# Cross-attention and quantised feed-forward, float32 on one core: the projection in two blocks side by side with 512-column matmuls, bias terms off TensorE, and another order on VectorE

## What is computed

```python
# x, ctx: (8, 256, 1024) float32
Q = layernorm(x) @ Wq.T + bq              # 1024 -> 1024
K = ctx @ Wk.T + bk
attn = softmax(Q @ K.T / sqrt(1024))      # within each of the 8 batches
x = x + attn @ ctx
w = scales[g_idx] * (where(nibble > 0, 1, -1) - zeros[g_idx])   # 1024 x 1024, from 4-bit codes
x = x + layernorm(x) @ w + bias
```

## Time and profile before

| | before |
|---|---|
| median of 3 runs | 609.89 us (607.79 to 610.23) |
| the profiled execution, its own time | 609.59 us |
| its span, first to last instruction | 607.8 us |
| TensorE busy | 584.0 us, 96% |
| VectorE busy | 380.8 us, 63% |
| ScalarE, GpSimd busy | 189.5 and 190.5 us, 31% each |
| HBM traffic, mean | 133 GB/s |

### The profile page before, as it was taken

The page is one execution under the profiler, slowest core; times in us unless marked ns, Lnnn a source line. Parts: engine busy times, 40 slices in busy tenths (PEclk is TensorE's granted clock), DMA queues, the critical chain, the costliest instruction groups (busy, mean ns, idle before and its releaser), DMA issues.

```text
span 607.8 us, 8093 instructions
## 1 busy us (share of the span) xinstructions
PE 584.0 (96%) x3098; PEld 501.0 (82%) x3098; DVE 380.8 (63%) x640; ACT 189.5 (31%) x346; POOL 190.5 (31%) x136
## 2 busy tenths in 40 slices
PE   7899999899999999989999999988899999999997
PEld 6799999687877877767889899977688888888886
DVE  4794885279678758845102555566787686777442
ACT  5312112210432332222326766654221222132120
POOL 3460000000000000000024877663856426624630
PEclk9999999899999999989999999999899999999999
DMA  8921200040180441405506599896203203310111
GB/s 272 294 71 35 71 1 2 0 139 1 70 310 36 174 173 69 157 19 189 189 3 243 209 324 354 316 420 271 116 2 139 111 39 128 139 70 0 70 69 70
DMA packets 30853, 81.47 MB, mean 134 GB/s; under 512 B 2600, under 2 KB 10800, under 8 KB 28640
## 3 DMA queue, kind: packets, MB, share of 16 engines
q1 hardware_dynamic: 30816, 80.96, 36.6%
HBM read 53.69 MB, written 27.26 MB: 133 GB/s over the span
## 4 chain that ended last, share of the span: by engine, by line
PE 82%; DVE 8%; DMA 3%; ACT 2%; POOL 2%; issue 1%; SPq 1%; DVEq 0%; ACTq 0%
PE bank L1029 25%; PE bank L1031 25%; PE bank L1030 25%; PE bank L1191 2%; PE bank L1040 2%; PE bank L1119 2%; DVE stats L734 1%; DMA wq_stage<-in_L_xattn_Wq 1%; DMA wk_stage<-in_L_xattn_Wk 1%; DVE xT_lo L685 1%; POOL cn_lo L444 1%; DVE wrow L713 1%; DMA xin<-in_x 1%; POOL tT_lo L451 1%; DVE yin L940 1%
## 5 line engine op out<-in xcount | busy, mean ns | idle before, releaser
L1029 PE MATMUL bank<-xT_hi,m_hi 128*128 128x512 f32 x256 | 106.3, 415 | 1.6 <-DVEq L787 1.6
L1030 PE MATMUL bank<-xT_lo,m_hi 128*128 128x512 f32 x256 | 102.1, 399 | 0.0
L1031 PE MATMUL bank<-xT_hi,m_lo 128*128 128x512 f32 x256 | 101.9, 398 | 0.0
L434 POOL TENSOR_TENSOR pairs<-mv,pairs 128x2 f32<-128x2 f32 x16 | 11.1, 695 | 208.2 <-DVE mv L739 207.5
L993 DVE TENSOR_TENSOR xres<-xres,bank 128x512 f32<-128x512 f32 x56 | 38.3, 686 | 48.3 <-PE bank L1031 48.2
L1029 PE MATMUL bank<-wk_hi,wq_hi 128*128 128x342 f32 x192 | 62.7, 327 | 4.9 <-DVE wk_lo L694 2.5
L466 POOL TENSOR_TENSOR l_lo_s<-l_sum_s,l_hi_s 128x512 fp32r<-128x512 f32 x32 | 40.4, 1296 | 73.3 <-DVE l_sum_s L922 71.8
L1030 PE MATMUL bank<-wk_lo,wq_hi 128*128 128x342 f32 x192 | 61.4, 320 | 0.0
L1031 PE MATMUL bank<-wk_hi,wq_lo 128*128 128x342 f32 x192 | 61.2, 319 | 0.0
L451 POOL TENSOR_TENSOR tT_lo<-t_pair,tT_hi 128x1024 fp32r<-128x1024 f32 x16 | 38.2, 2403 | 72.8 <-ACT tT_hi L490 72.8
L1029 PEld LDWEIGHTS bank<-xT_hi,m_hi 128*128 128x128 f32 x256 | 48.8, 190 | 14.0 <-DVEq L787 1.8
(11 more groups left out here) (138 smaller groups left out, 1299.7 us busy)
## 6 DMA issues: line engine op xcount, KB each, us to landing
xin<-in_x SPq DMA_DIRECT2D x8, 1024.0 KB, 6.3
cin<-in_ctx SPq DMA_DIRECT2D x8, 1024.0 KB, 6.8
xres<-in_x SPq DMA_DIRECT2D x8, 1024.0 KB, 11.6
out<-xres SPq DMA_DIRECT2D x15, 512.0 KB, 2.7
right_scratch<-part_hi SPq DMA_DIRECT2D x28, 256.0 KB, 2.2
r_tile<-right_scratch SPq DMA_DIRECT2D x6, 1024.0 KB, 11.4
r_tile<-right_scratch SPq DMA_DIRECT2D x3, 1536.0 KB, 10.1
right_scratch<-part_lo_t SPq DMA_DIRECT2D x16, 256.0 KB, 2.1
```

What stands on the lines that cost most here:

```text
L1029: pe.matmul(out_, a_hi, b_hi, start=start, stop=False, skip_group_check=True)
L1030: pe.matmul(out_, a_hi, b_lo, start=False, stop=False, skip_group_check=True)
L1031: return pe.matmul(out_, a_lo, b_hi, start=False, stop=stop, skip_group_check=True)
```

## The change

Blocks 0 and 1 of the projection run side by side: slice c of block 0, then slice c of block 1, so Wq's block 1 is loaded early and has buffers of its own; later blocks run one by one. M's rows are two segments of 512 columns; the banks go round by three pairs. Wk no longer has the bk columns. The bias terms: ScalarE multiplies each slice of Wk by bq (`times_bq`) into `wk_bq` and each block of Wq by bk (`times_bk`) into `wq_bk`; VectorE adds the eight slices (three wide additions) for u, and reduces each block (`sum_bk`) into `wacc` for w; `w_row` is two matmuls of 512 columns of float32. A slice of Wk from c = 4 on also waits for `times_bq` of slice c - 4. The second x load waits for blocks 0 and 1. In block 7 the x_tr are spread behind slices 3 to 7, and t's first group doesn't wait for `s_cons`; `w_row` does. In the t stage VectorE does `weights` before the six `x_lo`. On ScalarE `t_hi(2, 0)` moves behind two `c_hi`. At the turn `y_apply(0, 1)` moves up between the `c_lo(7, ...)`, `y_stats(1)` behind the loop, `left_sum` s3 and s4 and both `y_apply(1, ...)` between the residuals of batch 7, and `rsqrt(9)` on GpSimd behind the low parts of s2 and s1.

```diff
 SP:
-            first_wq(0, s_wq0)
+            first_wq(0, 0, s_wq0[0])
             for h, done in enumerate((s_wk0, s_wkl[0])):
...
+            first_wq(1, 0, s_wq0[1])
             for c in range(1, NB):
-                if c == 1:
+                if c == 2:
                     for r, row in enumerate((bq, bk)):
...
-                if c == 2:
-                    first_wq(1, s_wql[0])
+                if c == 3:
+                    for b in range(2):
+                        first_wq(b, 1, s_wql[b])
                 if c >= 4:
                     sp.wait_ge(s_wklo, c - 3)
+                    sp.wait_ge(s_wkbq, c - 3)
                 sp.dma_start(wk_stage[c % 4], wk_rows[:, c, :]).then_inc(s_wkl[c % 4], 16)
-            load_wq(1)
+            load_wq(2)
...
+            for b in range(3, NB):
+                sp.wait_ge(s_wqlo, wq_split_count(b - 3, 1))
+                sp.wait_ge(s_wqbk, b - 2)
                 load_wq(b)
+                if b == 3:
+                    sp.wait_ge(s_m, 4)
+                    sp.dma_start(xin[:, 1, :, :], x_rows[1]).then_inc(s_xl[1], 16)
 ScalarE:
+            def times_bq(c):
...
+                act.activation(wk_bq[:, c, :], wk_stage[c % 4], ACT.Copy, scale=bcols[:, 0, c:c + 1]).then_inc(s_wkbq, 1)
+            def times_bk(b):
+                wait(act, s_wacc, b)
+                for c in range(NB):
+                    ins = act.activation(wq_bk[:, c, :], wq_stage[b % 3][:, c, :], ACT.Copy, scale=bcols[:, 1, c:c + 1])
+                ins.then_inc(s_wqbk, 1)
...
             for c in range(1, NB):
                 if c == 3:
                     wq_split(0, 1)
+                    wq_split(1, 1)
                 act.wait_ge(s_wkl[c % 4], 16 * (c // 4 + 1))
+                copy(wk_hi[:, c, :], wk_stage[c % 4]).then_inc(s_wkhi, 1)
+                if c > 1:
+                    times_bq(c - 2)
+            times_bq(NB - 2)
+            times_bq(NB - 1)
+            times_bk(0)
...
-                if b + 1 < NB:
+                if b != 1 and b + 1 < NB:
                     for h in range(2):
-                        wq_split(b + 1, h)
+                        wq_split(max(b + 1, 2), h)
+                if b > 1:
+                    times_bk(b)
...
+                if b == 1:
+                    times_bk(b)
 VectorE:
+            dve.wait_ge(s_wkbq, NB)
+            order.link(dve.tensor_tensor(wk_bq[:, 0:4, :], wk_bq[:, 0:4, :], wk_bq[:, 4:8, :], ALU.add))
+            order.link(dve.tensor_tensor(wk_bq[:, 0:2, :], wk_bq[:, 0:2, :], wk_bq[:, 2:4, :], ALU.add))
+            dve.tensor_tensor(uacc, wk_bq[:, 0, :], wk_bq[:, 1, :], ALU.add).then_inc(s_uacc, 1)
             order.link(dve.tensor_tensor(jcol, bcols[:, 0, :], bcols[:, 1, :], ALU.mult))
             dve.tensor_reduce(bsum[:, 0:1], jcol, AX_X, ALU.add).then_inc(s_cons, 1)
-            def add_u(c):
...
+            def sum_bk(b):
+                dve.wait_ge(s_wqbk, b + 1)
+                dve.tensor_reduce(wacc[:, b * P:(b + 1) * P], wq_bk.rearrange("p c i -> p i c"), AX_X, ALU.add
+                                  ).then_inc(s_wacc, 1)
...
             for b in range(NB):
+                if b != 1 and b + 1 < NB:
+                    wq_split(max(b + 1, 2), 0)
...
+                if b != 1 and b + 1 < NB:
+                    wq_split(max(b + 1, 2), 1)
+                if b != 1:
+                    sum_bk(b)
                 if b == NB - 1:
-                    for u in range(4):
+                    for u in range(6):
                         x_lo(0, u)
+                for n in range(2):
+                    dve.wait_ge(s_mhi, 2 * b + n + 1)
+                    cols = slice(n * HALF, (n + 1) * HALF)
+                    low(m_lo[:, b, cols], m_bank(b, n)[:, :], m_hi[:, b, cols], s_mlo)
+                if b == 1:
+                    sum_bk(b)
...
                     n = NB * p + j
+                    for h in range(2):
+                        if n - 1 - h in GATHER:
+                            weights(GATHER[n - 1 - h], h)
                     if j == NB - 1 and p + 1 < PAIRS:
                         for u in range(NB - 2):
                             x_lo(p + 1, u)
...
                     if b == 1:
                         p_lo(0)
                         invert_sum(0)
+                    if b == B - 2:
+                        y_apply(0, 1)
                     c_lo(b + 1, 2)
                     c_lo(b + 1, 3)
...
                 row_max(b)
-                if b == B - 2:
-                    y_apply(0, 1)
-                if b == B - 1:
-                    y_stats(1)
...
-                if b == B - 1:
-                    y_apply(1, 1)
-                    y_apply(1, 0)
             p_lo(B - 1)
             invert_sum(B - 1)
-            dve.wait_ge(s_cnlo, 4 * B)
-            left_sum(0, "s3")
-            left_sum(0, "s4")
+            y_stats(1)
...
                 if f == 0:
                     added(f, 0)
                     added(f, 1)
-                    for g in range(4):
-                        residual(B - 1, g)
+                    dve.wait_ge(s_cnlo, 4 * B)
+                    left_sum(f, "s3")
+                    residual(B - 1, 0)
+                    left_sum(f, "s4")
+                    residual(B - 1, 1)
+                    y_apply(1, 1)
+                    residual(B - 1, 2)
+                    residual(B - 1, 3)
+                    y_apply(1, 0)
                     left_lo(f, "a22")
 TensorE:
+            for c in range(NB):
+                for b in range(2):
+                    proj(b, c)
+            for b in range(2, NB):
                 for c in range(NB):
+                    proj(b, c)
                     if b == NB - 1:
                         if c == 6:
                             u_sums()
+                        for u in {3: (0, 1), 4: (2,), 5: (3, 4), 6: (5,), 7: (6, 7)}.get(c, ()):
+                            x_tr(0, u)
...
-                        pe.wait_ge(s_cons, 3)
-                    if n == 1:
-                        pe.wait_ge(s_mlo, 3 * NB)
+                        pe.wait_ge(s_mlo, 2 * (NB - 1))
```

More of the change, by code:

```diff
@@ L508, in _ @@
                 copy(wk_hi[:, 0, cols], wk_stage[0][:, cols]).then_inc(s_wkhi, 1)
-            act.wait_ge(s_small, 32)
-            for i in range(2):
-                copy(wk_hi[:, :, D + i], bcols[:, 1, :]).then_inc(s_bks, 1)
+            wq_split(1, 0)
             for c in range(1, NB):
@@ L536, in _ @@
                     act.wait_ge(s_tbl, 2)
-                for n in range(3):
-                    act.wait_ge(s_m, 3 * b + n + 1)
-                    cols = slice(n * SEG, min((n + 1) * SEG, D))
-                    copy(m_hi[:, b, cols], bank[3 * (b % 2) + n][:, 0:cols.stop - cols.start]).then_inc(s_mhi, 1)
-            for u in range(4, NB):
-                x_hi(0, u)
+                for n in range(2):
+                    act.wait_ge(s_m, 2 * b + n + 1)
+                    copy(m_hi[:, b, n * HALF:(n + 1) * HALF], m_bank(b, n)[:, :]).then_inc(s_mhi, 1)
+                if b == 1:
+                    times_bk(b)
+            x_hi(0, 6)
+            x_hi(0, 7)
             for h in range(2):
@@ L657, in _ @@
                     if b == 1:
+                        t_hi(b + 1, 0)
                         p_hi(0)
@@ L687, in wq_split @@
             def wq_split(b, h):
-                cs = slice(4 * h, 4 * h + 4)
-                dve.wait_ge(s_wqhi, 2 * b + h + 1)
-                low(wq_lo[:, cs, :], wq_stage[b % 2][:, cs, :], wq_hi[:, cs, :], s_wqlo)
+                cs = slice(KH * h, KH * (h + 1))
+                dve.wait_ge(s_wqhi, wq_split_count(b, h))
+                low(wq_lo[b == 1][:, cs, :], wq_stage[b % 3][:, cs, :], wq_hi[b == 1][:, cs, :], s_wqlo)
             def wk_split(c, cols, n_hi):
@@ L697, in _ @@
             wq_split(0, 0)
-            wk_split(0, slice(0, HALF), 1)
+            wk_split(0, slice(0, HALF), 1).then_inc(s_wklo0, 1)
             wk_split(0, slice(HALF, D), 2).then_inc(s_wklo, 1)
-            dve.wait_ge(s_bks, 2)
-            for i in range(2):
-                low(wk_lo[:, :, D + i], bcols[:, 1, :], wk_hi[:, :, D + i], s_bks)
+            wq_split(1, 0)
             for c in range(1, NB):
@@ L858, in _ @@
                             x_lo(p + 1, u)
-                    for h in range(2):
-                        if n - 1 - h in GATHER:
-                            weights(GATHER[n - 1 - h], h)
                     if n + 1 in GATHER:
@@ L1085, in w_row @@
             def w_row():
-                pe.wait_ge(s_wcol, NB)
-                pe.wait_ge(s_mlo, 3 * NB)
-                for n in range(NB):
-                    ins = pe.matmul(bank[4 + n // 4][:, n % 4 * P:(n % 4 + 1) * P],
-                                    wcol[:, n:n + 1].broadcast_to([P, P]), ident, start=True, stop=True)
-                    if n % 4 == 3:
-                        ins.then_inc(s_wr, 1)
+                pe.wait_ge(s_wacc, NB)
+                pe.wait_ge(s_cons, 3)
```

(3 more changed lines are left out.)

168 lines of the change are left out of this document (81 added, 87 removed).

## The result

| | before | after |
|---|---|---|
| median | 609.62 us (606.39 to 614.14, 20 runs) | 614.77 us (612.75 to 618.46, 20 runs) |
| the profiled execution | 609.59 | 613.37 |
| its span | 607.8 | 611.6 |
| ratio after/before | | 1.009 [1.0068, 1.0111] |

The change made the kernel slower by 0.9%. 612.6 was forecast, in a range of 601 to 617. The two profiled executions differ by 3.8 us, the medians by 5.2.

The account below looks back on a forecast made before the run. TensorE, busy 584.0 of 607.8 us, was taken as the bound, with idle gaps and low clock as losses. +9.0 + 1.7 - 1.0 - 4.8 - 4.7 - 0.2 + 3.0 = +3.0 gave 612.6 us, range 601 to 617.

Parts of the forecast that it names:

- A: Start of the projection: block 2 begins at 45.2 instead of 36.2 us, behind the bq sums; +9.0, bounds +1.9 and +10.5.
- C: End of the projection: 2.6 us of idle time and 1.7 of clock go; -4.8, or -3.1 if the clock falls.
- F: The turn: first yin waits for rstd, later gaps go, work returns before the fifth product; +3.0, bounds -1.5 and +3.8.
- my walk: Steps at the start: slice 7's low part ready at 27.0, blocks 0 and 1 ended at 30.3, undisturbed sums at 38.1.
- The clock behind it: Behind the gap of 15 us ahead of block 2, TensorE's clock is low: +1.7 us.
- B: Projection blocks 2 to 7: a block takes 11.16 instead of 11.35 us, the bk work hidden; -1.0 us.
- D: VectorE's order at group 23: weights ahead of six xT_lo remove the 2.98 us gap and its low clock; -4.7.
- E: t_hi(2, 0) behind c_hi: transposes come 1 us sooner, but the next matmul waits for pT_lo anyway; -0.2 us.
- Rival 1: The bq sums at the start meet no GpSimd work; block 2 starts at 38.1, total 605.5 us; chance 0.18.
- Rival 3: VectorE sets the turn: it waits for GpSimd, clock falls twice; F +5.5, A at its upper end, 617 us; chance 0.10.
- Rival 2: The bq chain at the start is short; block 2 at 32 to 34, total 598 to 601 us; chance 0.12.
- rival 4: The turn gains because rstd is early; F = -1.5, total 608 us; chance 0.10.

## Why the prediction was right, and where it was wrong

The time came out 2.2 us above the forecast and inside the range. The difference of the profiled executions was closer still, +3.8 against +3.0, but that is in part luck: two of the terms were off, A by -2.4 and C by +4.0, and nearly cancelled. (The lower end of 605 that the prediction gives for its terms is that of A alone; with F's as well it is 601.)

- **A, the start: right in mechanism, in this profile too long by 2.4** (+6.6 for +9.0). The long gap, ended by `wq_lo` behind three sums, with GpSimd's instructions between, is there: 12.07 us. Slice 7's low part (made at 26.95), the end of blocks 0 and 1 (30.73) and the undisturbed end (38.00 in the run with late tables) fell within half a microsecond of my walk. The turns of GpSimd cost 4.8 us here, where I took 7.1 of bounds 6.6 and 8.6. I had put a wait of 1.4 to 2.0 ahead of nearly each VectorE instruction; over their undisturbed durations they took 1.6, 0.7, 1.9 and, the low part, 0.8 longer. Not foreseen: slice 7 lands at another time in other executions. In four runs whose start is that of the changed kernel its copy came at 26.5 to 27.8 instead of 24.62, and block 2 began at 45.9 to 46.8. There A is +9.7 to +10.6, over the forecast and up to its upper bound of +10.5, once just past it. From slice 7's copy to block 2 it takes 18.2 us in the profile of after, 18.6 to 19.4 in those four and 13.2 with the tables late, so the turns cost 5.0 to 6.2. That fits the median lying 1.4 us above the profiled execution; what delays the loads I did not test.
- **The clock behind it: right**, 1.9 us by the window, 1.7 forecast. **B: right.** The first products with bk of two successive blocks start 90.01 - 78.86 = 11.15 us apart, forecast 11.16. The product with bq takes 1.14 (1.06 taken), eight products with bk 2.44, hidden in the middle of a block as I said. The reduce takes 1.9 to 2.0, not 1.2.
- **C, the end of the projection: wrong.** I forecast -4.8 and it gave -0.8. The failed step is "xT_lo of six tiles is made by then". In B I had costed the bk products and reduces at nothing because both engines are idle half of a block. In block 7 that cover is gone: the x parts have to be made within the block, and two products of 2.44 and two reduces of about 2.0 us stand ahead of them in one chain. A gap of 2.43 and 1.6 us of clock took the place of those removed. The run with the last product moved gives the 3.9 back. In the four traces in which the clock stayed high behind that gap, C is -2.4.
- **D: right**, -4.7, and shown alone.
- **E: right**, -0.2: the +1.6 ahead of it is +1.4 at the product that waits for pT_lo (338.12 against 336.74).
- **F, the turn: right in its steps, too long by 0.6.** `residual(5, 0)` is late for rstd, +1.7 with +1.9 forecast, once the 1.4 us that after is late there are taken off; of the gaps of 2.96 and 2.11 0.18 is left; the work comes back ahead of the fifth product, behind a gap of 2.73 with 3 forecast. At the fifth product it is +0.8 (2.1 forecast), with 1.6 of clock behind it, so +2.4 instead of +3.0. The work ahead of the fifth product was priced 1.3 too high; of the clock behind it, "perhaps 1.7", the +3.0 holds about half, and 1.6 came.
- **The rivals.** Rival 1, no GpSimd work beside the sums, gave 605.5; made on purpose it gives 610.1, which is 4.7 under after: it lacks the 4.0 of C. Rival 3 did not come in full: the clock fell twice, but the waits for GpSimd were those of the forecast. Its condition, rstd later than 403.7, did hold. Rival 2 (block 2 at 32 to 34) and rival 4 (F = -1.5) did not come: block 2 began at 42.8 to 46.8 in the five traces with this start, and F was +2.4.

## What to carry to other kernels

When TensorE is 96% busy, work taken off it is worth only what it leaves on the path: here 204 matmuls less gave 1 us (B), and the bias work that moved to VectorE and ScalarE left a wait of 12, which put block 2 back by 6.6 to 10.6. Work that is free in the middle of a stage has to be costed again at its first and last block, with the buffer it goes through. Before a long reduction is put at the end of a load, see whether it can be added while the load runs; and when a wait is moved, price the next consumer down the same queue too.

## What was not expected of the hardware

The granted clock does not fall behind each gap of the same length. At pv(5) the gap is 3.48 us in the changed kernel and 3.49 in the run with rstd(9) early, in the same place with the same work ahead:

```profile
414.70 0.50 PE L1066 MATMUL bank<-cn_hi,pT_hi 128*128 128x512 f32 x1 [3.49 <-DVE xres L940]
```
```profile
404.00:430.00 26.00, 22.46 (x146) 19.67 (x145) 14.19 (x22) 11.54 (x28) 16.68 (x11) 1.00 0.77 306
```

The clock is 1.00 there and 0.93 in the changed kernel. By distances it shows at three places where other runs have the same work and the same gap. From the product behind the gap of 3.5 us at pv(5) to the first with `l_hi_a` it takes 15.45 us here, 16.6 to 16.9 in three traces and 17.9 to 18.0 in two. Behind the gap of 2.4 in block 7 the clock costs nothing in four traces and 1.6 us in three. Behind the gap of 2.73 at the fifth product it costs nothing in three and 1.6 in four. So a gap of 2.4 to 3.5 us costs its length, and in some executions 1.2 to 2.6 us more. A difference of that size between two single traces does not show what an edit does.

Even a tiny VectorE instruction waits for GpSimd: jcol, 8 elements, took 2.08 us beside GpSimd (0.99 in other runs) and 0.16 without it. The Trainium skill (SBUF — State Buffer, Who interferes with whom) has a VectorE instruction with two SBUF inputs contend with a GpSimd instruction that reads SBUF, with the issue order and not the shape deciding who waits. The runs agree: jcol has two inputs, and it ends just behind GpSimd's instruction. The reduce of one input, 1024 float32 read with a stride, takes 1.9 to 2.0 us, where an addition of as many takes 1.23.
